# DMA transposes for half of the output, first sizes made on ScalarE, and kernel products two channels earlier

## What is computed

```python
dt = exp(log_dt); A = -exp(log_A_real) + 1j * A_imag
dtA = A * dt[:, None]
P = dtA[:, :, None] * arange(length)
Cs = Cc * (exp(dtA) - 1.0) / A
K = 2.0 * einsum('hn,hnl->hl', Cs, exp(P)).real        # (64 channels, 1024)
y = irfft(rfft(u * mask, 2 * L) * rfft(K, 2 * L))[..., :L]
y = (y + u * mask * D[:, None]) * mask
```

```python
gate = x2 @ Wg; up = x2 @ Wu                            # weights unpacked, minus zeros, times scales
inter = gate * sigmoid(gate) * up
out = x + (inter @ Wd).astype(float16)
```

## Time and profile before

| | |
|---|---|
| median of 3 runs | 1173.37 us (1173.34 to 1173.43) |
| the profiled execution | 1176.32 us, span 1174.4 us |
| TensorE matmul busy | 1149.5 us, 98% of the span |
| VectorE busy | 887.7 us, 76% |
| ScalarE busy | 847.5 us, 72% |
| GpSimd busy | 222.0 us, 19% |
| DMA | 173.94 MB, mean 148 GB/s |

### The profile page before, as it was taken

How to read it: one execution, slowest core, us unless ns; L and a number is a source line. 1 busy time by engine, 2 the same in 40 slices (tenths; PEclk the granted TensorE clock), 3 DMA queues, 4 the chain that set the end, 5 groups by cost and what they waited for, 6 DMA issues and landing times.

```text
span 1174.4 us, 15087 instructions
## 1 busy us (share of the span) xinstructions
PE 1149.5 (98%) x5562; PEld 954.5 (81%) x5562; DVE 887.7 (76%) x985; ACT 847.5 (72%) x1398; POOL 222.0 (19%) x139
## 2 busy tenths in 40 slices
PE   5999999999999999999999999999999999999996
PEld 5999998788888888888888888888888888888883
DVE  7678745677777777777777988887777777777775
ACT  6443204887888788788788797777888887888873
POOL 0122000211422422211111252111211211211213
PEclk8999999999999999999999999999999999999999
DMA  7878778441653556434434875455344334444514
GB/s 282 283 229 254 238 263 222 111 108 27 159 138 99 150 147 178 109 87 121 115 81 118 261 186 143 152 180 160 91 108 120 96 108 111 105 108 108 152 53 163
DMA packets 66976, 173.94 MB, mean 148 GB/s; under 512 B 11654, under 2 KB 17222, under 8 KB 66902
## 3 DMA queue, kind: packets, MB, share of 16 engines
q1 hardware_dynamic: 64834, 171.14, 50.7%
q10 hardware_dynamic: 2036, 1.81, 0.5%
q0 software_dynamic: 32, 0.03, 0.0%
HBM read 159.94 MB, written 15.83 MB: 150 GB/s over the span
## 4 chain that ended last, share of the span: by engine, by line
PE 94%; DMA 2%; DVE 2%; issue 1%; POOL 0%; ACT 0%; SPq 0%; DVEq 0%; POOLq 0%
PE pair L1257 28%; PE pair L1298 27%; PE pair L1278 27%; PE pair L1211 11%; DMA toep<-kernel_padded 1%; PE pair L1170 1%; PE pair L1191 0%; DMA kernel_padded<-k_sb 0%; POOL o L590 0%; PE pair L1327 0%; PE pair L1360 0%; DMA logs<-in_L_cond_log_dt_dram 0%; PE pair L1347 0%; PE pair L1338 0%; DVEq L175 0%
## 5 line engine op out<-in xcount | busy, mean ns | idle before, releaser
L1023 DVE SCALAR_TENSOR_TENSOR acc<-pair,s_down,acc 128x1024 f32<-128x1024 f32 x328 | 420.3, 1283 | 189.7 <-PE pair L1298 189.3
L703 ACT ACTIVATE pair<-pair,ratio 128x512 f32<-128x512 f32 x616 | 382.3, 665 | 101.4 <-PE pair L1257 101.2
L722 ACT ACTIVATE pair<-pair,ratio 128x512 f32<-128x512 f32 x581 | 360.7, 659 | 117.8 <-PE pair L1278 117.7
L1257 PE MATMUL pair<-high,wg 128*128 128x512 f32 x704 | 278.6, 396 | 0.0
L1257 PE MATMUL pair<-low,wg 128*128 128x512 f32 x704 | 277.1, 394 | 0.0
L1298 PE MATMUL pair<-mid_h,wd 128*128 128x512 f32 x688 | 268.2, 392 | 0.0
L1298 PE MATMUL pair<-mid_l,wd 128*128 128x512 f32 x672 | 265.7, 395 | 0.0
L1278 PE MATMUL pair<-high,wu 128*128 128x512 f32 x672 | 265.0, 394 | 0.0
L1278 PE MATMUL pair<-low,wu 128*128 128x512 f32 x672 | 264.0, 393 | 0.0
L542 POOL CAST mid_h<-sil 128x1024 fp32r<-128x1024 f32 (+1 forms) x43 | 45.2, 1052 | 694.5 <-DVE sil L1000 684.0
L1257 PEld LDWEIGHTS pair<-high,wg 128*128 128x128 f32 x704 | 132.1, 188 | 31.3 <-ACT pair L703 1.1
(11 more groups left out here) (150 smaller groups left out, 589.9 us busy)
## 6 DMA issues: line engine op xcount, KB each, us to landing
q_in<-rows_backwards SPq DMA_DIRECT2D x86, 512.0 KB, 4.6
z_in<-zeros_plus_one SPq DMA_DIRECT2D x130, 256.0 KB, 4.7
toep<-kernel_padded SPq DMA_DIRECT2D x64, 512.0 KB, 6.7
q_in<-_L_ffn_down_qweight_dram SPq DMA_DIRECT2D x42, 512.0 KB, 4.8
u_all<-in_x_dram SPq DMA_DIRECT2D x13, 512.0 KB, 10.9
x_fin<-in_x_dram SPq DMA_DIRECT2D x12, 512.0 KB, 9.3
out_dram<-x_fin SPq DMA_DIRECT2D x12, 512.0 KB, 5.6
high_parts<-staged SPq DMA_DIRECT2D x8, 512.0 KB, 2.9
```

The costliest lines, as they stand in the source:

```text
L703: act.activation(gate_ps[:, tb, :], gate_ps[:, tb, :], ACT.Copy, scale=ratio[:, 0, G * t + g:G * t + g + 1]).then_inc(gate_scaled, 1)
L722: act.activation(up_ps(tau)[:, tb, :], up_ps(tau)[:, tb, :], ACT.Copy, scale=ratio[:, 1, G * t + g:G * t + g + 1]).then_inc(up_scaled, 1)
L1023: dve.scalar_tensor_tensor(out=acc[:, hid, :], in0=ps, scalar=scale, in1=acc[:, hid, :], op0=ALU.mult, op1=ALU.add).then_inc(down_taken, 1)
L1257: mm = pe.matmul(gate_ps[:, tb, :], w["g"][tau % 2][:, g, :], rows[:, g, 512 * tb:512 * tb + 512], start=g == 0 and part == 0, stop=part = ...
```

## The change

Five edits.

1. The first half's output is transposed by DMA. `turn_out`, `turns_before` and `turn_at` are gone. SyncE, from tau 25 on, issues four DMA transposes in each of eight steps of tau (32 in all, each of 128 x 256 f16 from `o16` to a new buffer `turned`), then stores and loads rows of x in the same function. VectorE's `finish` handles one block of rows at slots 1 and 3 of tau 26, 28, 30 and 32, and reads `turned` in SBUF.
2. The sizes of the first two chunks are made on ScalarE straight from the exponent table, eight exponentials of 64 elements with the parameter as scale. VectorE first copies a quarter of `par_ps`, makes the first angles from the accumulator, and then copies the other three quarters.
3. ScalarE copies the first block of x ahead of the first sine; the second half of block 5 is transposed after the first kernel product.
4. Kernel products of chunks 3 to 8 stand ahead of the second channel of their group.
5. SyncE loads the Toeplitz slices of a group ahead of the first weights.

```diff
@@ sync
                 if chunk_begun_at(g - 2) is not None:
                     store_kernels(chunk_begun_at(g - 2))
+                load_toeplitz(g + 2)
                 if g == NG - 4:
                     sp.wait_ge(k_mm, NCH)
 ...
                     load_weights("u", 0)
-                load_toeplitz(g + 2)
 ...
+            def turn_and_store(v):
+
+                j, part = divmod(v, 2)
+                if v == 0:
+                    sp.wait_ge(o16_done, NH)
+                elif part == 0:
+                    sp.wait_ge(out_ready, 2 * j)
+                    for tt in (2 * j - 2, 2 * j - 1):
+                        store_out(0, tt)
+                if j < 4:
+                    for hid in range(4 * part, 4 * part + 4):
+                        sp.dma_start_transpose(turned[:, :, P * hid:P * hid + P], o16[:, hid, 2 * P * j:2 * P * j + 2 * P]
+                                               ).then_inc(rows_turned, 16)
+                if part and j in (1, 2):
+                    for tt in (2 * j + 2, 2 * j + 3):
+                        sp.wait_ge(out_stored[tt % 4], 16)
+                        load_x(0, tt)
 ...
+                if TURN_FROM <= tau <= TURN_FROM + HALF_G:
+                    turn_and_store(tau - TURN_FROM)
@@ scalar
+            take_rows(0, 1)
             act.wait_ge(first_args, 1)
 ...
-            take_rows(0, 3)
-            sizes(1, 0, 8)
-            act.activation(warm[:], ident[:, 0:1], ACT.Sin)
-            take_rows(3, 4)
+            take_rows(1, 3)
+            act.activation(warm[:, 1:2], ident[:, 0:1], ACT.Exp)
+            act.wait_ge(par_copied, 1)
+            for h in range(8):
+                act.activation(size[:, h, :], tab[:, C_B:C_B + 64], ACT.Exp, scale=par[:, 0, h:h + 1]
+                               ).then_inc(first_sizes, 1)
+            act.activation(warm[:, 0:1], ident[:, 0:1], ACT.Sin)
+            take_turned(3, 0)
             angles(0)
+            take_turned(3, 1)
@@ vector
+            dve.wait_ge(tab_in, 16)
             dve.wait_ge(par_turned, 1)
-            do(dve.tensor_copy(par[:], par_ps[:, 0:4 * H].rearrange("p (v h) -> p v h", v=4)))
+            dve.tensor_copy(par[:, 0], par_ps[:, 0:H]).then_inc(par_copied, 1)
+            theta_0 = bass.AP(par_ps.tensor, par_ps.offset + H, [par_ps.ap[0], [1, 4], [0, 64]])
+            do(dve.tensor_tensor(theta[:, 0:4], theta_0, bass.AP(tab[:].tensor, C_B, [[C_N, P], [0, 4], [1, 64]]), ALU.mult))
+            dve.tensor_copy(par[:, 1:4], par_ps[:, H:4 * H].rearrange("p (v h) -> p v h", v=3)).then_inc(par_copied, 1)
 ...
+            def finish(tt):
+
+                dve.wait_ge(rows_turned, 16 * NH * (tt // 2 + 1))
+                dve.wait_ge(x_fin_in[tt % 4], 16 * (tt // 4 + 1))
+                to = x_slot(0, tt)
+                dve.tensor_tensor(to, turned[:, tt % 2], to, ALU.add).then_inc(out_ready, 1)
 ...
-            exp_sizes(0, 0, 8)
-            turn_angles(0)
             reduce_angles(0)
+            dve.wait_ge(par_copied, 2)
 ...
+                    if g in (1, 3) and tau > TURN_FROM and (tau - TURN_FROM) % 2 and tau < TURN_FROM + HALF_G:
+                        finish(tau - TURN_FROM - 1 + g // 2)
@@ tensor
-            for g in range(3, 6):
+            for g in range(3, 5):
                 turn(g)
+            turn(5, (0,))
 ...
-                    if hh == 3 and chunk_begun_at(g - 2) is not None:
+                    if hh == 1 and chunk_begun_at(g - 2) is not None:
                         multiply_kernel(chunk_begun_at(g - 2))
 ...
             multiply_kernel(0)
+            turn(5, (1,))
 ...
-                    if TURN_AT <= n < TURN_AT + 4 * TURN_STEP and (n - TURN_AT) % TURN_STEP == 0:
-                        turn_out((n - TURN_AT) // TURN_STEP)
```

## The result

The changed kernel takes **1189.16 us** (median of 6 runs, 1183.88 to 1190.66) against 1173.40 us of the kernel before beside it (6 runs, 1172.89 to 1178.68): ratio **1.0119**, 95% interval 1.0094 to 1.0144. It is slower, by 15.8 us between the medians. The ratio is one of means (14.0 us apart here), and three stray executions of the experiments (1776, 2951 and 4049 us) are left out of the ratios. The forecast was 1184.9 us in a range of 1178.0 to 1190.5.

What follows compares the result with a forecast made beforehand. The prediction took TensorE, 94% of the chain, and its semaphore waits as the bound. Its terms, -3.8 + 12.3 + 5.1 - 2.0 - 0.1 = +11.5 us on the median 1173.37 us, gave 1184.9 us, range 1178 to 1190.5.

Steps and rivals of the forecast that it cites:

- The products: Convolution, chunks 3 to 8: TensorE asks 4.6 us earlier and waits for VectorE's L897, +12.3 us.
- GpSimd's part: Chunks 5 and 6: GpSimd's subtraction slows L897 from 0.42 to 2.46 us; 4.0 of the 12.3 us hang on it.
- The clock: Convolution: half clock behind the new holes at chunks 5, 6 and 7, 1.7 us each, +5.1 us (bounds 0 to 9.3).
- The transposes: Feed-forward: four turn_out calls of 0.96 us leave TensorE for DMAs on SyncE's queue, -3.8 us.
- Their cover: DMA transposes at tau 26: four need 6.4 to 13.4 us of 10.9 us available; no cost taken.
- The Toeplitz hole: Group 14 of the convolution: TensorE's 1.96 us wait for its slices goes, by later product and load order, -2.0 us.
- The head: Start of the kernel: first product 0.65 us earlier, convolution start between 0.25 us later and 0.7 us earlier, taken as -0.1 us.
- The sum: Whole kernel: all terms together +11.5 us, put on the median of the runs, 1184.9 us.
- no term hangs on that difference: Whole kernel: profiled span 1174.4 us against median 1173.37 us affects no term, so the sum goes on the median.

Runs made afterwards that it cites:

- experiment 2: The kernel before with one edit alone, products of chunks 3 to 8 ahead of the second channel: 1189.88 us, ratio 1.0119.
- experiment 3: The changed kernel with unread matmuls filling TensorE's long holes ahead of the products of chunks 5, 6 and 7: 1183.39 us, ratio 1.0062.
- experiment 1: The changed kernel with the products of chunks 3 to 8 back at the fourth channel: 1169.94 us, ratio 0.9940.
- experiment 11: The changed kernel with the products back at the fourth channel, same code as experiment 1, run once more: 1170.79 us, ratio 0.9961.
- experiment 5: The changed kernel with GpSimd's subtraction of groups 5 and 7 held back until VectorE finished left and right of chunks 5 and 6: 1182.57 us, ratio 1.0053.
- experiment 6: The kernel before with the DMA transposes of the first half's output alone: 1170.37 us, ratio 0.9958.
- experiment 7: The kernel before with the edits of the head alone (sizes on ScalarE, par copies, half a block's transposes moved): 1174.15 us, ratio 0.9997.
- experiment 8: The kernel before with one edit, a group's Toeplitz slices loaded ahead of the first weights: 1174.38 us, ratio 0.9990.
- experiment 9: The changed kernel with products at the fourth channel and all eight DMA transposes of a pair in its second step: 1169.84 us, ratio 0.9949.
- experiment 10: The changed kernel with products at the fourth channel and unread matmuls ahead of the first two kernel products: 1168.53 us, ratio 0.9947.
- experiment 4: The changed kernel with the products of chunks 3 to 8 ahead of the third channel: 1175.77 us, ratio 0.9994.
- experiment 12: The kernel of experiment 9 with SyncE also waiting for a gate product before issuing the DMA transposes: 1190.86 us, ratio 1.0141.

## Why the prediction was right

**What bounds the kernel.** TensorE and its waits, as said. Every microsecond of the difference but the last store is in TensorE's timeline.

**The products.** Forecast 12.3 us, found 12.47 in the five waits of the convolution. One by one: chunk 5 4.35, found 4.30; chunk 6 2.9, found 2.85; chunk 7 3.55, found 3.45; chunk 8 0.9, found 0.84; chunk 4 none. Chunk 3 was 0.4 and came as 1.03, and there the step missed something small: the wait of group 2 for its Toeplitz slice, 0.36 us, had been excusing VectorE, and it was absent in this execution. In experiments 2 and 3 the two shared the time otherwise (0.52 and 0.27; 0.17 and 0.59). Request against completion, from one trace, was enough for this, because nothing in the change moves VectorE's turns against TensorE's. That wait of group 2 differs between executions of one kernel (0.79 us in experiment 1, 1.09 in experiment 11), so a few tenths of this agreement are chance. Experiments 1 and 2 show that this edit carries the whole loss.

**GpSimd's part.** The forecast took the two slow L897 as they were the earlier trace rows; they came again (2.45 us beside 2.54 us of GpSimd), and experiment 5 removed them.

**The clock.** Forecast 5.1 us in bounds of 0 to 9.3; the stage table leaves 5.9, experiment 3 gives 5.9, and the stretches 6.4. The mechanism and the places were right, the size was short: three falls of 1.7 us were assumed, and the third lasted twice as long, at 1.2 GHz for 6.8 us from 148.85 us on. The reason given, that TensorE is in full work on both sides, doesn't tell the short stretch from the long one. By the Trainium skill (TensorE: Matmul & The Clock Gate, Part 1) an idle TensorE is put back to half rate; experiment 3 agrees in the sense that the same waits with TensorE busy cost no clock.

**The transposes.** Forecast -3.8 us, found -3.5, in the changed kernel and in experiment 6 alike: the chain's 0.96 us for a call was 0.88 us, one fourth of the difference between additions 178 and 210. At the faster pace of TensorE that the last section shows it is 4.3 us: 92.16 us between them in experiments 7 and 8, which keep turn_out, and 87.89 in experiments 9 and 10. Their cover held with more to spare than said. The issue was assumed at 0.6 us like a load's; it was 1.25 us, and the landing of 4 to 11 us was 2.3 to 6.1. Four take 3 x 1.25 + 2.4 = 6.2 us, a little under the short end of the bounds (6.4), of the 11.4 us from 759.64 to 771.03 (the prediction had 10.9). The two errors cancelled. The estimate worked out from the Trainium skill (VectorE: DVE Perf Modes, The three transpose paths) was 10.5 us for these four; the trace has 6.2 us, so the measurement decides. VectorE's addition took 1.21 to 1.22 us in all eight instances, and GpSimd's subtraction had ended 0.5 us before the four that it was near to: they never met, and zero was right, but what a meeting would cost here wasn't tested.

**The Toeplitz hole.** Forecast -2.0 us, found -1.96. The two causes given together, the product and the order, are each enough (experiments 2 and 8). In executions where the wait is 1.3 us the gain is only that.

**The head.** Forecast -0.1 us, found 0.0, and 0.9997 alone. Not because nothing changed: ScalarE's eight sizes took 2.02 us behind a wait for VectorE, the first angles began at 19.88 us, and the first product at 22.25 in place of 22.31. The 0.65 us that VectorE gave up were lost again on ScalarE:

```profile
15.98 2.02 ACT L644 ACTIVATE size<-tab,par 128x64 f32<-128x64 f32 x8 [0.85 <-DVE par L857]
18.01 1.28 ACT L646 ACT_TABLE_LOAD   x1
...
19.88 0.42 ACT L610 ACTIVATE arg<-arg 128x256 f32<-128x256 f32 x1
```

**The sum.** The parts found, +12.5 + 5.9 - 3.5 - 2.3 + 0.0 = +12.6 us, are the 12.6 us between the spans, with 1.1 us of faster pace and 1.2 us of a longer last store cancelling. The forecast's own sum was 11.5, so its parts and their errors (0.8 of the clock the largest) come out well. The measured median is another matter: it lies 4.3 us above the forecast and 1.3 us under the end of the range. What was missed is the step that put the sum on the median, "no term hangs on that difference". The medians are 15.8 us apart, 3 us more than the traces, and the means 14.0.

Why isn't shown, since only one execution of each kernel has a trace. Two things that differ between executions are of this size. One is a pace of TensorE, shown in the last section; the six times of before (1172.9 to 1173.4, with others at 1175.3 and 1178.7) would fit it. The other is the clock: the mean granted clock of the changed kernel was 0.991 in the traced execution, 0.992 in the fastest (1183.88 us) and 0.986 to 0.988 in the four others. Lower by 0.005 over 1187 us is some 12 us more at half clock, and up to 6 us lost, if TensorE had work in that time. So the forecast's clock term, 5.1 us, may have been further off in most executions than the traced one shows.

## What to carry to other kernels

When a consumer is moved ahead, compare for each instance the time at which it will ask with the end of its producer; here two views and six subtractions gave the sum of the waits to 0.2 us. A hole in TensorE's stream costs its own length and may cost nearly as much again at half clock (3.45 us and some 3 us behind it in the changed kernel); filling it with idle work takes the second part back (5.9 us for the three). Work moved off the bounding engine is a gain only up to its own room, so measure that room by making it late once: here 2.9 us, of which the change used nothing.

## What the runs showed of the hardware

**When the clock falls isn't settled by the length of the hole.** In the convolution, 2.00 us (experiment 4) and 2.29 us (experiment 5) brought no fall, 2.85 us did in the changed kernel and didn't in experiment 2, and 3.45 us and more always did (in the changed kernel and in experiments 2, 5 and 12, nine holes of 3.45 to 4.59 us, the last four of them in the feed-forward stage). Behind the same 3.45 us hole the slow stretch was 6.8 us in the changed kernel and in experiment 5, but 3.4 us in experiment 2. The 2.01 us in the head of before did coincide with a slow stretch. What else decides stays open.

**TensorE has more than one pace at the same granted clock.** VectorE's additions 218 and 339, some 15 tau apart, in experiment 11:

```profile
809.02 1.28 DVE L1038 SCALAR_TENSOR_TENSOR acc<-pair,s_down,acc 128x1024 f32<-128x1024 f32 x1
...
1139.07 1.28 DVE L1038 SCALAR_TENSOR_TENSOR acc<-pair,s_down,acc 128x1024 f32<-128x1024 f32 x1 [0.57 <-PE pair L1309]
```

and in experiment 10, with the same feed-forward code:

```profile
808.32 1.28 DVE L1038 SCALAR_TENSOR_TENSOR acc<-pair,s_down,acc 128x1024 f32<-128x1024 f32 x1
...
1135.14 1.28 DVE L1038 SCALAR_TENSOR_TENSOR acc<-pair,s_down,acc 128x1024 f32<-128x1024 f32 x1 [0.54 <-PE pair L1317]
```

330.05 against 326.82 us, 1% on every tau (22.19 and 21.97 us), with a granted clock of 1.00 in both. The traces of before, of after and of experiments 1 to 6 and 11 have the slower pace there, those of experiments 7 to 10 the faster, whatever the kernel; in experiment 12 a tau took 22.19 us ahead of the four waits and 21.97 behind the last, so the pace can change within an execution. It moves the time by 3 us here and by 4.4 over the whole feed-forward stage (955.53 and 951.15 us), more than the transposes do, and fits the spread of the 32 runs of the kernel before beside experiments 5 to 8 (1171.0 to 1177.9 us). Its cause wasn't looked for. A gain of this size has to be read stage by stage, or from many runs.

**A DMA transpose of 128x256 f16 within SBUF** took SyncE's queue 1.25 us to issue (the median, up to 2.6 us), twice a load's 0.59 us, and had landed 2.3 us after its start at the earliest.
